# VectorE's other instructions of a step, each behind one undivided slot of a recurrence, and the first norm's statistics ahead of the second's

## What is computed

```python
x = x + conv(_ln_c(x))              # first norm, over 192 channels of each token
t = tokens(x)                       # 8 x 256 tokens of 192 channels
t = t + ffn(_ln_t(t))               # second norm, over the same 192 channels

# conv: DeltaNet, 12 heads of 16, chunks of 16 tokens; h is the normed token
q, k = l2norm(silu(h @ Wq)), l2norm(silu(h @ Wk))
v, beta = silu(h @ Wv), sigmoid(h @ Wb)
# per head, token after token:  u = beta (v - S^T k);  S = S + k u^T;  o = S^T q
conv = h + o @ Wo

# ffn: 8 routed experts of 192 hidden channels, the best two of each token, and a shared one of 768
gates, idx = top_k(softmax(t @ router_w), 2)      # gates divided by their sum
ffn = alpha * shared + (1 - alpha) * routed       # alpha = sigmoid(t @ sg_w + sg_b)
```

## Time and profile before

| | us |
|---|---|
| median of 3 runs | 486.1 |
| lowest and highest | 484.05, 486.39 |
| span of the profiled execution, first to last instruction | 484.3 |
| VectorE busy | 416.6 (86%) |
| TensorE busy | 416.3 (86%) |
| GpSimd busy | 412.6 (85%) |
| ScalarE busy | 352.6 (73%) |

### The profile page before, as it was taken

How to read it: one execution, slowest core, us unless ns; L and a number is a source line. 1 busy time by engine, 2 the same in 40 slices (tenths; PEclk the granted TensorE clock), 3 DMA queues, 4 the chain that set the end, 5 groups by cost and what they waited for, 6 DMA issues and landing times.

```text
span 484.3 us, 10459 instructions
## 1 busy us (share of the span) xinstructions
PE 416.3 (86%) x2400; PEld 383.9 (79%) x2400; DVE 416.6 (86%) x2290; ACT 352.6 (73%) x1035; POOL 412.6 (85%) x527
## 2 busy tenths in 40 slices
PE   1445265899999999999999999999999989999996
PEld 0323144798898999999999989898989889899895
DVE  4259889999999999999999999999999999996200
ACT  3699366587878787787869696969696847485862
POOL 5478698999999999999999999999999999986340
PEclk9999999999999999999999999999999999999999
DMA  6568383633242323223232323322332232300301
GB/s 165 162 131 169 92 163 90 146 93 111 50 118 70 97 65 91 72 89 84 70 84 87 91 83 83 92 81 71 92 102 69 74 99 73 98 3 1 115 1 16
DMA packets 43437, 42.91 MB, mean 89 GB/s; under 512 B 20144, under 2 KB 35184, under 8 KB 43376
## 3 DMA queue, kind: packets, MB, share of 16 engines
q1 hardware_dynamic: 42768, 42.05, 33.2%
q10 hardware_dynamic: 608, 0.21, 0.2%
HBM read 35.95 MB, written 6.29 MB: 87 GB/s over the span
## 4 chain that ended last, share of the span: by engine, by line
DVE 41%; PE 24%; POOL 10%; issue 8%; ACT 8%; SPq 6%; DMA 3%; POOLq 0%; ACTq 0%; DVEq 0%
DVE Pr L1378 9%; DVE bank L1382 9%; DVE u L1380 8%; DVE SH L1386 7%; PE bank L454 5%; POOL PQ L932 3%; POOL PQ L925 3%; ACT L733 3%; PE bank L427 2%; PE bank L439 2%; PE bank L431 2%; PE bank L429 2%; PE bank L430 2%; PE bank L428 2%; POOL hid L970 2%
## 5 line engine op out<-in xcount | busy, mean ns | idle before, releaser
L970 POOL TENSOR_TENSOR hid<-sg,ug 128x192 f32<-128x192 f32 x192 | 112.9, 607 | 22.4 <-ACT ug L699 19.0
L925 POOL TENSOR_TENSOR PQ<-SH,QB 128x768 f32<-128x768 f32 x62 | 112.8, 1841 | 0.4 <-DVE SH L1386 0.4
L932 POOL TENSOR_TENSOR PQ<-PQ 128x768 f32<-128x768 f32 (+2 forms) x93 | 103.0, 1107 | 6.1
L454 PE MATMUL bank<-Wd,hidT 128*128 128x192 f32 x576 | 106.6, 326 | 0.0
L698 ACT ACTIVATE sg<-bank 128x192 f32<-128x192 f32 x192 | 63.6, 331 | 58.3 <-PE bank L431 48.3
L1382 DVE TENSOR_TENSOR bank<-bank,u 128x96 f32<-128x96 f32 (+1 forms) x467 | 104.2, 264 | 0.1
L1378 DVE TENSOR_TENSOR Pr<-SH,bank 128x96 f32<-128x96 f32 (+1 forms) x437 | 100.8, 265 | 3.5 <-PE bank L394 1.3
L1380 DVE TENSOR_REDUCE u<-Pr 128x6 f32<-128x102 f32 (+1 forms) x437 | 102.3, 268 | 0.6 <-issue 0.2
L1386 DVE TENSOR_TENSOR SH<-SH,bank 128x96 f32<-128x96 f32 (+1 forms) x467 | 101.7, 254 | 0.3
L454 PEld LDWEIGHTS bank<-Wd,hidT 128*128 128x128 f32 x576 | 94.5, 190 | 0.0
L427 PE MATMUL bank<-Whi,hiT 128*128 128x384 f32 (+1 forms) x192 | 73.6, 383 | 1.3 <-DVE loT L1134 1.1
(11 more groups left out here) (147 smaller groups left out, 817.0 us busy)
## 6 DMA issues: line engine op xcount, KB each, us to landing
QB<-q_scratch SPq DMA_DIRECT2D x64, 384.0 KB
k_scratch<-khl SPq DMA_DIRECT2D x64, 48.0 KB, 1.7
KR<-k_scratch SPq DMA_DIRECT2D x32, 96.0 KB, 2.4
q_scratch<-qn SPq DMA_DIRECT2D x64, 24.0 KB, 1.6
Wd<-in_L_ffn_w_down_dram SPq DMA_DIRECT2D x4, 288.0 KB, 8.9
out_dram<-xT SPq DMA_DIRECT2D x1, 896.0 KB, 4.1
Wlo_unsplit<-in_L_ffn_w_gate_dram SPq DMA_DIRECT2D x2, 384.0 KB, 4.5
Wlo_unsplit<-in_L_ffn_w_up_dram SPq DMA_DIRECT2D x2, 384.0 KB, 5.4
```

What stands on the lines that cost most here:

```text
L454: last = mm(bDn[:, 0:C], hidT[:, turn_half(g), k - lo, :], Wd[:, k, :], start=False, stop=(k == KT - 1))
L925: tt(PQ[:, at * BR * HP:(at + n) * BR * HP].rearrange("p (i b h) d -> p i b (h d)", i=n, b=BR), SH[:, lo:lo + n].rearrange("p i b h d -> p ...
L932: chained(tt(PQ[:, :, 0:w], PQ[:, :, 0:w], PQ[:, :, w:2 * w], ALU.add))
L970: tt(hid[:, r * H:(r + 1) * H], sg[:, m % RING], ug[:, m % RING], ALU.mult).then_inc(s_hid, 1)
```

## The change

The set of undivided slots grows from 16 to 27. On VectorE, for the steps 1 to 15, the other instructions get new slots: the first norm's statistics stand behind the slots 25, 26 and 27 (before: 30, 31, 32), the second's behind 32, 33 and 34 (before: all behind 32), A_vT behind 36 (before 37), Fa_bias behind 38 (before 36), the two halves of Fa_split behind 43 and 44 (before: both behind 43), A_ss behind 45 (before 44) and A_bias behind 46 (before 52). On TensorE, A_x stands ahead of Fa_o and of `fill` 4 (before: behind both). Nothing that is computed changes.

```diff
-WHOLE = frozenset((9, 31, 32, 37, 44, 48, 49, 50, 51, 52, 53, 54, 55, 56, 57, 58))
+WHOLE = frozenset((8, 9, 19, 23, 25, 26, 27, 32, 33, 34, 36, 38, *range(43, 52), *range(53, 59)))
@@ TensorE, steps 1 to 15
                     at(-2, Fb_up, 6)
                     at(-3, Fb_down, 4)
+                    at(3, A_x)
                     at(-1, Fa_o)
                     at(0, fill, 4)
-                    at(3, A_x)
                     at(-2, Fb_turn, 0)
                     at(-1, Fa_y)
@@ VectorE, steps 1 to 15
                         at(23, -1, Fa_otok)
-                        at(30, 3, A_stats)
-                        at(31, 3, A_mean)
+                        at(25, 3, A_stats)
+                        at(26, 3, A_mean)
+                        at(27, 3, A_var)
                         at(32, -1, Fa_stats)
-                        at(32, -1, Fa_mean)
-                        at(32, 3, A_var)
-                        at(32, -1, Fa_var)
-                        at(36, -1, Fa_bias)
-                        at(37, 1, A_vT)
+                        at(33, -1, Fa_mean)
+                        at(34, -1, Fa_var)
+                        at(36, 1, A_vT)
+                        at(38, -1, Fa_bias)
                         at(43, -1, Fa_split)
-                        at(43, -1, Fa_split_tail)
-                        at(44, 2, A_ss)
+                        at(44, -1, Fa_split_tail)
+                        at(45, 2, A_ss)
+                        at(46, 3, A_bias)
                         at(47, -1, Fa_logits)
                         at(47, -1, Fa_max)
                         at(48, -1, G_dif, done)
                         at(49, -1, G_eq, done)
                         at(50, -1, G_gt, done)
                         at(51, -1, G_rank, done)
-                        at(52, 3, A_bias)
                         at(53, -1, G_sel, done)
```

## The result

The changed kernel takes 505.4 us in the median (503.43 to 505.84), the kernel before 485.6 in the runs beside it: a ratio of 1.040, with an interval from 1.037 to 1.043. The forecast was 494.1 us in a range up to 497.5: right in the sign, too small by more than half. The profiled execution has a span of 504.1 us against 484.3. (Rows 4 to 7 lie in the steps c = 8 and 9; their titles count one less.)

What follows compares the result with a forecast made beforehand. The prediction took a round of ScalarE and TensorE, 25.43 us a step, as the bound. Ten steps by 0.70 us plus 0.5 and 0.5 gave +8.0; 484.3 + 8.0 + 1.8 = 494.1 us, range 487.5 to 497.5.

Steps and rivals of the forecast that it cites:

- The round of ScalarE and TensorE: Kernel before: L653 to copy L709 7.70 us, to TensorE 0.74, to L355 12.21, to next L653 4.78; 25.43 us a step.
- The rival that VectorE's saving would come through: VectorE is the limit and its 0.7 us a step come through: 476 to 478 us, chance 0.08.
- VectorE's way from A_x to L653: L355 through A_stats and Fa_bias to L653: 5.88 us where 5.18 are free, each step 0.70 us longer.
- ScalarE waited at L653 for Fa_bias: Sign on ScalarE: a wait for VectorE's L1122 ahead of L653, 0.3 to 0.7 us.
- the first Fb_up: TensorE, after Fa_split: comes 0.75 us later, covered by the 0.8 us wait at L439; uncovered, 0.75 us a step.
- A_x's new place: TensorE, A_x ahead of Fa_o and fill 4: its L355 comes 0.40 us earlier.
- 0.40 + 5.24 + 0.24 priced: L355 to A_stats 0.40, A_stats to Fa_bias 5.24, Fa_bias to L653 0.24: 5.88 us in all.
- the price of the merged slots: VectorE: 0.065 us saved per merged slot with enough work behind; without any, 0.07 us lost; sum 0.7 us a step saved.
- lose 0.7 us: VectorE's work a step: 0.39 us from six merged slots, some 0.2 from spread statistics, 0.1 from slots 36 to 38.
- 1.0 and 0 us: Steps 1 and 2 each +0.5 us; at the end, +0.3 of longer stretch and -0.3 of VectorE's savings cancel.
- The sign that was named for being wrong: VectorE not waiting for L355 ahead of L1085; a wait of 0.5 to 1 us was forecast in steps 2 to 12.
- The rival on the slow side: A_x waits for v and doesn't get its 0.40 us: 0.95 to 1.1 us a step, 497 to 499 us, chance 0.07.

Runs made afterwards that it cites:

- the covered kernel: Changed kernel, moves kept, with undivided slots only where entered behind another instruction or an undivided slot (9, 26, 27, 33, 34, 44 to 58): 493.6 us, ratio 1.017.

## Why the prediction was wrong

**What bounds the kernel: right.** The round of ScalarE and TensorE set the 25.43 us; moving one copy out of it shortened the profiled step, by 0.12 us. The rival that VectorE's saving would come through fell: it had no saving.

**Where the path goes: right in the main.** VectorE's way from A_x to L653 took the round over (in the changed kernel VectorE's lengthened list stands beside it within 0.05 us), ScalarE waited at L653 for Fa_bias, the first Fb_up came late without cost, and A_x's new place gave its 0.40 us. With every slot covered, the terms give the step to 0.02 us, part of it by luck: 0.40 + 5.24 + 0.24 priced, 0.31 + 5.41 + 0.24 measured, 26.13 against 26.15 us.

**The step that failed: the price of the merged slots**, "a merged slot saves about 0.065 us only with 0.13 us or more of other work behind it". It asks what stands behind an undivided slot, and not what stands ahead of it. The earlier trace rows has an undivided slot with an instruction on either side (255.50 to 255.90); no row shows one entered from a divided slot with nothing between, and I took 0.33 us for that as if it were shown. A bound was to be had: the two halves of a slot start 0.17 us apart and an undivided instruction needs the second, so the entry is up to 0.2 us late. It measured 0.19 us, nine times a step, 1.7 us. VectorE's list didn't lose 0.7 us; it grew by about 1, from 25.3 to 26.2 us without waits.

This one term enters the sum in two places:

- A_stats to Fa_bias has three such entries (32, 36, 38): 5.77 us where 5.24 were priced. With L355 to A_stats at 0.34 instead of 0.40, the step is 26.55 us, not 26.13. Ten steps: 12 us instead of 7, single stalls included.
- Up to step 2 and in the steps 12 to 15 the round over A_x doesn't decide, and VectorE's list does. I had set its saving against the longer stretch and got 1.0 and 0 us; they are 3.7 and 4.4. The run with the slots 8, 19, 23 and 43 divided again gave back 2.8 and 2.2 of them; the covered kernel has -0.8 and +0.7 us there.

**The sign that was named for being wrong** ("if VectorE doesn't wait at L1085") was there: the list was so long that VectorE came to A_stats just when A_x was ready.

**The range** was wrong for the same reason. The rival on the slow side was A_x waiting for v, up to 499 us; that VectorE's list might grow was no case at all, since I took fewer instructions to be a gain, or at worst nothing.

## What to carry to other kernels

Before merging two independent halves of a dependent chain, look at both neighbours of the merged instruction: what is ahead of it must cover the second half's latency, what is behind it must cover its own. Run undivided slots together and begin each run behind an instruction that is there anyway. In a kernel whose busiest engines are all within a few per cent of full, write down each round over two or three engines with its sum: here two rounds and VectorE's own list lay between 25.1 and 25.43 us, an edit that shortens the longest buys at most the distance to the next, and one that lengthens any of them costs all that goes beyond its distance to the longest, 0.1 to 0.3 us here.

## What the runs showed of the hardware

The busy time hides the loss. At an uncovered entry VectorE stands still for only 0.10 us (254.02 to 254.12 above), and the list of waits doesn't show it: the kernel with the new undivided slots alone shows VectorE 25.72 us busy in a step of 26.75 and no wait of note. Only the distance from start to start tells.

The clock column can read 1.00 where the matmuls run at half. The kernel before shows a granted clock of 1.00 from 60 to 80 us, the changed one 0.50; the first line is of before, the second of the changed kernel:

```profile
60.00:80.00 20.00, 12.20 (x33) 8.09 (x33) 18.32 (x102) 14.05 (x35) 18.84 (x19) 1.00 0.62 138
```

```profile
60.00:80.00 20.00, 12.24 (x33) 8.39 (x33) 17.58 (x88) 13.17 (x33) 18.57 (x18) 0.50 0.64 141
```

But the same matmuls start 0.33 us apart in both (lines L428 and L429 of step 1, before and changed), which is the lower level, 1.2 GHz; in the kernel before they start 0.18 us apart in step 8 (254.09 to 254.27):

```profile
76.19 0.53 PE L428 MATMUL bank<-Wlo,hiT 128*128 128x394 f32 x1
76.52 0.53 PE L429 MATMUL bank<-Whi,loT 128*128 128x394 f32 x1
```

```profile
77.59 0.53 PE L428 MATMUL bank<-Wlo,hiT 128*128 128x394 f32 x1
77.92 0.53 PE L429 MATMUL bank<-Whi,loT 128*128 128x394 f32 x1
```

So the mean clock of 0.946 in the changed kernel's profile is no cause of its time: both kernels begin at the lower level, and over the seven steps of the earlier trace rows and the seven shown of the changed kernel (148.68 to 334.53 us) the granted clock is 1.00 in both.
